# A 16-sequence attention and mixture-of-experts kernel on one core: three tiles combined to two turns of groups, the shared expert and the last routing steps placed elsewhere

## The reference

```python
x = x + attention(layernorm(x))        # 16 heads of 64, over 256 tokens, softmax, + bo
z = layernorm(x)
probs = sigmoid(z @ router_w.T + expert_bias)            # 160 experts
top_w, top_idx = top_k(probs, 8)
top_w = 2.5 * top_w / (sum(top_w) + 1e-09)
routed = sum over the 8 chosen e of  top_w[e] * (silu(z @ w_gate[e].T) @ w_down[e].T)   # inner size 64
shared = silu(z @ w_gate_shared.T) @ w_down_shared.T
out = x + routed + shared
```

## Time and profile before

| | us |
|---|---|
| median of 3 runs | 1121.14 |
| lowest and highest | 1119.48, 1123.74 |
| the profiled execution | 1122.37 |
| its span in the profile | 1120.5 |
| busy: PE, DVE, ACT, POOL | 868.7, 794.1, 703.0, 704.9 |
| granted PE clock, mean | 0.893 of full speed |

### The profile page before, as it was taken

One profiled execution on the slowest core, in us unless ns is written; L12 is line 12 of the kernel. 1 busy time (PEld: TensorE's weight loads), 2 busy tenths in 40 slices (PEclk: granted clock), 3 DMA queues, 4 the chain that ended last, 5 costly groups with the idle time before them and its releaser, 6 DMA issues.

```text
span 1120.5 us, 30801 instructions
## 1 busy us (share of the span) xinstructions
PE 868.7 (78%) x8800; PEld 673.4 (60%) x8800; DVE 794.1 (71%) x2741; ACT 703.0 (63%) x2069; POOL 704.9 (63%) x892
## 2 busy tenths in 40 slices
PE   5999999999999999999999977887775757700000
PEld 4777777777777778777777756665554535500000
DVE  4568888888888888888878888787775666743223
ACT  5888888888888888888888745764443434500000
POOL 2236676767767676776767755277555454577775
PEclk9999999999999999999999968998887887855555
DMA  8715644444443122312222446886665666522221
GB/s 266 313 59 225 261 164 162 176 183 183 173 184 109 63 94 68 104 60 103 70 75 84 143 155 214 261 284 218 213 202 166 189 197 190 177 61 54 61 56 49
DMA packets 75566, 170.00 MB, mean 152 GB/s; under 512 B 13809, under 2 KB 23985, under 8 KB 75505
## 3 DMA queue, kind: packets, MB, share of 16 engines
q1 hardware_dynamic: 56816, 133.63, 33.9%
q0 software_dynamic: 16384, 33.59, 10.4%
q10 hardware_dynamic: 2304, 2.10, 0.6%
HBM read 66.50 MB, written 102.76 MB: 151 GB/s over the span
## 4 chain that ended last, share of the span: by engine, by line
PE 61%; DVE 12%; POOL 10%; issue 10%; DVEq 5%; ACT 1%; DMA 0%; POOLq 0%; ACTq 0%
PE psS L419 12%; PE psO L494 11%; PE psT L444 9%; PE psY L410 9%; POOL yg L909 9%; DVE w_b L1253 6%; PE psVM L410 5%; PE psA L456 5%; DVEq L249 3%; PE psS L603 3%; PE psT L593 3%; PE psY L614 2%; DVE yg L1260 2%; DVEq L1253 1%; DVE yg L1262 1%
## 5 line engine op out<-in xcount | busy, mean ns | idle before, releaser
L909 POOL DMA_INDIRECT yg<-block_y,tok_idx x256 | 249.8, 976 | 167.2 <-issue 93.7
L883 POOL DMA_INDIRECT slot_x<-xn_src,slot_u x240 | 246.1, 1025 | 97.2 <-issue 54.8
L712 ACT ACTIVATE p_sb<-psS,negmax 128x256 f32<-128x256 f32 x512 | 236.0, 474 | 92.5 <-DVE negmax L1195 91.2
L1253 DVE COPY w_b<-w_all 128x192 f32 x832 | 171.0, 277 | 88.8 <-issue 49.4
L845 POOL TENSOR_SCALAR p_sb<-p_sb,rinv 128x256 f32<-128x256 f32 x256 | 137.3, 544 | 115.3 <-DVE rinv L1150 111.6
L1195 DVE TENSOR_REDUCE negmax<-psS 128x2 f32<-128x512 f32 x256 | 164.3, 683 | 28.6 <-PE psS L419 28.4
L419 PE MATMUL psS<-qk_sb 64*128 64x256 f32 x1024 | 145.2, 402 | 2.3 <-ACT p_sb L712 2.3
L494 PE MATMUL psO<-pT_sb,v_sb 128*64 128x256 f32 x1024 | 138.8, 390 | 4.1 <-issue 2.2
L287 ACT COPY pT_sb<-psT 128x512 f32<-128x512 f32 x256 | 140.9, 618 | 1.4 <-PE psT L444 1.4
L593 PE MATMUL psT<-ident,xb 128*128 128x128 f32 x416 | 80.2, 324 | 71.2 <-DVE x_res L1242 69.2
L444 PE MATMUL psT<-ident,p_sb 128*128 128x128 f32 x1024 | 132.7, 272 | 0.0
(11 more groups left out here) (164 smaller groups left out, 1796.5 us busy)
## 6 DMA issues: line engine op xcount, KB each, us to landing
block_y<-zero SPq DMA_DIRECT2D x26, 1024.0 KB
xb<-slot_x SPq DMA_DIRECT2D x104, 256.0 KB
block_y<-y_b SPq DMA_DIRECT2D x104, 256.0 KB
slot_x<-zero SPq DMA_DIRECT2D x15, 1024.0 KB, 4.0
w_all<-in_wgd_dram SPq DMA_DIRECT2D x16, 960.0 KB
slot_x<-zero SPq DMA_DIRECT2D x1, 11264.0 KB, 41.7
yg<-block_y,tok_idx POOLq DMA_INDIRECT x256
slot_x<-xn_src,slot_u POOLq DMA_INDIRECT x240
```

The source lines that it names most:

```text
L712: act.activation(p_sb[:, (g - 1) % 2, h, qt, :], psS[:, h, qt * SEQ:(qt + 1) * SEQ], ACT.Exp, bias=negmax[:, (g - 1) % 2, h, qt:qt + 1], s ...
L883: pool.indirect_dma_start(slot_x, bass.IndirectOffsetOnAxis(ap=slot_u[:, int(last), i, j:j + 1], axis=0), (xn2 if last else xn2_src)[:, i, ...
L909: pool.indirect_dma_start(yg[:, r, k, :], None, block_y, bass.IndirectOffsetOnAxis(ap=tok_idx[:, par, r, k:k + 1], axis=0)).then_inc(gat[r ...
L1253: m = dve.tensor_copy(w_b[:, RING - 1 - r, i, :], w_all[:, bass.ds(e, 1), :].rearrange("p o i -> p (o i)"))
```

## The change

`TILES_BY` says how many tiles are combined by the end of each turn from turn 10 on: 1, 3, 4, 6, ... 24. So turns have one and two `combine` in alternation, 24 are inside the turns and 8 behind them. All of DVE's turns from 7 on, and SP's from 8 on, are written out. The shared expert moves: `shared_hidden` to the turn's first group, `shared_out` to its second, DVE's `shared` behind the weights of the third group of the same turn, and PE's wait for it to the transposes of the third. SP's load of the shared expert's input comes a turn earlier. The last sequence's `chosen`, `best_places`, `blocks` and `weights` go from behind groups 7, 8 and 9 to behind groups 28 to 31; its table half from behind group 13 to behind group 33 (`LATE_TABLE`). `output_rows` now works on one sequence's 16 numbers per partition at a time, at step g = 6 of attention, with own small arrays; its last two calls come behind `ffn_norm(B)` and behind group 32. POOL's first gather waits only until 15 sequences have their row numbers; the third tile waits for the last sequence's row numbers and weights. In memory the tensors that the late steps still need lie where the third and fourth place of `yg` come.

```diff
+TILES_BY = [3 * j // 2 for j in range(TURNS - COMBINE_FROM + 1)]
-LEAD, LATE_RANKS, LATE_TABLE = 4, 5, 13
+LEAD, LATE_RANKS, LATE_TABLE = 4, 5, 33
...
-                    if r == 0 and chunk is not None:
-                        wait(pe, s["shared_ok"], chunk)
-                    if r == RING - 1 and chunk is not None:
+                    if r == 1 and chunk is not None:
                         pe.wait_ge(s["hs_ok"], chunk + 1)
+                    if r == 2 and chunk is not None:
+                        pe.wait_ge(s["shared_ok"], chunk + 1)
...
-                    if r == RING - 2 and chunk is not None:
+                    if r == 0 and chunk is not None:
                         shared_hidden(chunk)
-                    if r == RING - 1 and chunk is not None:
+                    if r == 1 and chunk is not None:
                         shared_out(chunk)
...
-            pool.wait_ge(s["wr_ok"], B)
-            pool.wait_ge(s["po_ok"], 3)
+            pool.wait_ge(s["po_ok"], SEALED + 1)
...
+                if isinstance(n, int) and n == 2:
+                    pool.wait_ge(s["wr_ok"], B)
+                    pool.wait_ge(s["po_ok"], B)
...
+            def output_rows(b):
+                n = b - 1
+                slot = slot_u[:, int(is_last(b, 2))]
                 wait(dve, s["su_ok"], n)
-                dve.tensor_copy(pos_u[:, bass.ds((b - 2) * TB, TB), :], slot_u[:, int(is_last(b, 2))]).then_inc(s["pu_ok"], 1)
+                dve.tensor_scalar(row_a[:], slot, 3, 6, ALU.bitwise_and, ALU.logical_shift_left).then_inc(s["pa_ok"], 1)
...
+                dve.tensor_tensor(pos_u[:, bass.ds((b - 2) * TB, TB), :], row_a[:], row_c[:], ALU.bitwise_or).then_inc(s["po_ok"], 1)
...
                         if g == 5:
                             weights(b)
+                        if g == 6:
+                            output_rows(b)
...
-                    if r == 0 and chunk is not None:
+                    if r == 2 and chunk is not None:
                         shared(chunk)
...
+            with dve.Fori(LEAD, COMBINE_FROM - 3) as it:
+                turn(it)
+            group(28)
             chosen(B + 1)
+            group(29)
             best_places(B + 1)
-            group(8)
+            group(30)
             blocks(B + 1)
-            group(9)
+            group(31)
             weights(B + 1)
-            group(10)
-            output_rows()
-            group(11)
-            group(12)
-            group(13)
+            group(32)
+            output_rows(B + 1)
+            group(33)
             dve.wait_ge(s["b_ps"], 2)
             table(psT[:, (LATE_TABLE - 1) % 2, :], TABLE_A, BC)
...
+            turn(COMBINE_FROM - 1, 0)
+            for j in range(TURNS - COMBINE_FROM):
+                turn(COMBINE_FROM + j, j + 1 if j + 1 < B else None)
+                for n in range(TILES_BY[j], TILES_BY[j + 1]):
+                    combine(n, n // YR, n % YR)
+            with dve.Fori(TILES_BY[-1] // YR, NT // YR) as q:
                 for k in range(YR):
                     combine(YR * q + k, q, k)
```

More of the change, by code:

```diff
@@ L135, in build @@
             newest = sa("newest", [P, E])
+            xn2T = sa("xn2T", [D, SEQ])
+            z_sb = sa("z_sb", [P, TB, E])
+            repl = sa("repl", [P, TB, E])
+            moved = repl
+            mask = sa("mask", [P, TB, E], BF16)
+            n_taken = sa("n_taken", [P, 1])
+            st2 = sa("st2", [P, TB, 6])
+            mv2 = sa("mv2", [P, TB, 2])
+            ve2 = sa("ve2", [P, TB])
+            rs2 = sa("rs2", [P, TB])
+            half = sa("half", [P, TB])
+            d = sa("d", [P, TB + 1, E])
+            le = d
+            taken = sa("taken", [P, E])
             placed = sa("placed", [P, TB, E])
+            score = sa("score", [P, TB, E])
             blk_num = sa("blk_num", [P, BC])
@@ L209, in build @@
         blk_i = sb("blk_i", [P, NBLK], I32)
+        tok_idx = sb("tok_idx", [P, 2, YR, TOPK], U32)
         w_all = sb("w_all", [P, E, INTER + D])
[L212 to L213 removed]
         xs = xn2_src[:].rearrange("p i d -> p (i d)")
@@ L357, in turn @@
                     store_y(RING * it + (r - STORE_LAG), (r - STORE_LAG) % 2)
-                    if r == 1 and chunk is not None:
-                        wait(sp, s["sh_ps"], chunk)
-                        sp.dma_start(xs, xT[bass.ds(chunk, 1)].rearrange("o p t -> (o p) t")).then_inc(s["xs_in"], 16)
+                if chunk is not None:
+                    wait(sp, s["sh_ps"], chunk)
+                    sp.dma_start(xs, xT[chunk]).then_inc(s["xs_in"], 16)
             xT = ffn_xT.rearrange("(b p) t -> b p t", p=D)
@@ L379, in _ @@
             sp.wait_ge(s["x2_st"], 16 * B)
[L380 to L392, removed]
+            for c in range(2):
+                turn(COMBINE_FROM - 2 + c, c)
+            for j in range(TURNS - COMBINE_FROM):
+                turn(COMBINE_FROM + j, j + 2 if j + 2 < B else None)
+                for n in range(TILES_BY[max(j - 1, 0)], TILES_BY[j]):
+                    store_out(n, n % YR)
             for n in range(NGRP - STORE_LAG, NGRP):
                 store_y(n, n % 2)
-            store_out(TURNS - COMBINE_FROM - 1, YR - 1)
-            with sp.Fori((TURNS - COMBINE_FROM) // YR, NT // YR) as q:
+            for n in range(TILES_BY[-2], TILES_BY[-1]):
+                store_out(n, n % YR)
+            with sp.Fori(TILES_BY[-1] // YR, NT // YR) as q:
                 for k in range(YR):
@@ L662, in _ @@
                 experts(it)
-            with pe.Fori(LEAD, COMBINE_FROM - 1) as it:
+            with pe.Fori(LEAD, COMBINE_FROM - 3) as it:
+                experts(it)
+            for it in range(COMBINE_FROM - 3, COMBINE_FROM - 1):
                 experts(it)
@@ L1284, in _ @@
             ffn_norm(B)
+            output_rows(B)
             dve.wait_ge(s["b_ps"], 1)
@@ L1318, in _ @@
             dve.wait_ge(s["tab_ok"], 2)
-            group(14)
-            group(15)
-            with dve.Fori(LEAD, COMBINE_FROM) as it:
-                turn(it)
-            for k in range(YR):
-                turn(COMBINE_FROM + k, k)
-                combine(k, 0, k)
-            with dve.Fori(1, (TURNS - COMBINE_FROM) // YR) as q:
-                for k in range(YR):
-                    turn(YR * q + (COMBINE_FROM + k), YR * q + k)
-                    combine(YR * q + k, q, k)
-            with dve.Fori((TURNS - COMBINE_FROM) // YR, NT // YR) as q:
+            group(34)
+            group(35)
+            turn(COMBINE_FROM - 1, 0)
+            for j in range(TURNS - COMBINE_FROM):
+                turn(COMBINE_FROM + j, j + 1 if j + 1 < B else None)
+                for n in range(TILES_BY[j], TILES_BY[j + 1]):
+                    combine(n, n // YR, n % YR)
+            with dve.Fori(TILES_BY[-1] // YR, NT // YR) as q:
                 for k in range(YR):
```

56 lines of the change are left out of this document (20 added, 36 removed).

## The result

The changed kernel takes 1074.76 us (median of 4 runs, 1074.22 to 1077.73), beside 1120.31 for the kernel before (4 runs): ratio 0.9597, 95% interval 0.9565 to 0.9629. The profiled execution has a span of 1072.4 us, where 1057 was forecast, and a mean granted clock of 0.912 (before 0.893). The time is inside the range of 1050 to 1076, by 1.2 us, and 17 us above the forecast of 1058.

The account below looks back on a forecast made before the run. POOL's gathers, waiting for DVE's sums, were taken as the bound. Tile 5 at 770.5, 275.4 for 27 tiles and 7.0 give 1052.9; 2 for attention and 2 for turns make 1057, median 1058 us, range 1050 to 1076.

Parts of the forecast that it names:

- rival (a): DVE's turns take above 15.1 us and set the end; about 1069 us at 16 a turn; chance 0.15.
- PE's waits for `x_res`: Sign: PE's waits for DVE's `shared` fall from 69.2 to under 30 us.
- A first gather near 714: Sign: POOL's gathers start near 714 us instead of 720.4.
- if a gather takes over 1.3 us: Sign that the prediction is wrong: a POOL gather over 1.3 us, where each took about 0.94.
- What bounds the kernel: POOL's gathers set the end, losing 67 us to waits for the sum of the tile four before.
- The first groups: Groups 7 to 13: moved steps save 6.2 us, table half 1.2, `output_rows(B)` costs 1.0; gathers start at 714.0.
- Attention: `output_rows` at g = 6 of 14 sequences: nothing or 0.6 us each, 8 us; 2 taken.
- The turns: DVE's turns: 12.1 us with one combine, 15.2 with two, mean 13.7, below POOL's 15.3.
- The sum: Tile 5 starts at 770.5; 27 tiles at 10.2 us are 275.4, plus 7.0 behind the last gather: 1052.9.
- (b): Groups 7 to 11 are bound elsewhere, gathers start at 719 to 720: 1061 to 1063 us; chance 0.07.
- (c): DVE's longer attention loop gets a gap at 11 jumps back, adding 44 us: 1100; chance 0.03.
- (d): POOL's gathers slow down beside DVE's copies, end near 1243 at the slowest gather seen; chance 0.02.

Follow-up runs that it names:

- g2_late_early: Changed kernel with the last sequence's steps and table half back behind groups 7 to 13; 1079.88 us, 0.9606 of the kernel before.
- g4_rows_only: Kernel before, with only `output_rows` on one sequence at a time at step 6 of attention; 1121.49 us, 0.9981 of the kernel before.
- f2_rows_behind_copy: Changed kernel with `output_rows` behind DVE's copy of psO at the end of step 5, second chip; 1072.25 us, 0.9527 of the kernel before.
- f3_no_multiply: Changed kernel without the multiplication by the routing weights in `combine`, second chip; 1064.02 us, 0.9465 of the kernel before.
- f4_all_three: Changed kernel with rows behind the copy, `combine` as eight multiply-adds, POOL written out without `tok_idx` copies; 1053.23 us, 0.9371 of the kernel before.
- e1_rows_behind_copy: Changed kernel with `output_rows` behind the copy of `oT_sb` in attention, on the slow first chip; 1269.99 us, 0.9901 of the kernel before.
- f1_after_again: Changed kernel as it is, run again on the second chip; 1073.79 us, 0.9546 of the kernel before.

## Why the prediction was right and where it was off

*The number.* That the time is in the range is in part luck. The forecast's own range was 1050 to 1064, and it was missed; 1064 to 1076 had been held open for the nearer half of rival (a), turns above 15.1 us, and they were 13.1. Of the signs that were named, PE's waits for `x_res` and the missing 5 us jumps of DVE came true. A first gather near 714, 10.2 us a tile and attention at most 3 us longer did not, and "if a gather takes over 1.3 us" was to show the prediction wrong: 18 of the 19 long ones do. That sign was badly chosen, as the 1989 ns of the earlier trace rows were there before.

*What bounds the kernel.* Right. POOL waited for the sum of the tile four before; with the sums early it runs almost without a wait for DVE from tile 6 to the end.

*The first groups.* Right: 7.9 us against 7.4; `g2_late_early` gives 6 for them at the first gather, and 5 to 6 at the end. `output_rows(B)` took 1.06 us (row 654.46 to 655.52 of DVE), 1.0 was taken. Not forecast were 1.7 us behind group 16, where loads for PE come late, and 2.0 more up to the first gather.

*Attention, the first step that failed.* "Bounds: nothing, or 0.6 each, 8 us. I take 2." The traces show 0.52 a sequence and 6.4 to 6.5 us from the first mask to the last, near the upper bound. PE full "means that it has work ahead" was the wrong reading, since a later maximum made every sequence longer. `g4_rows_only` gives 6.2 us for this step alone. Behind the copy 6.0 us are gone (`f2_rows_behind_copy`), of which 1.5 at most reach the end.

*The turns.* Right, and a little better than forecast: 12.1 and 15.2 us were given, mean 13.7; measured are 13.1 for the mean, and 11.2 with one combine. The third tile had its cover: `output_rows` ends at 737.2, its gather starts at 745.16. PE's waits for `x_res` fell to 18.2.

*The sum, the second step that failed.* "Tiles 5 to 31 are 27 x 10.2." The pace came from the earlier trace rows behind 991 us, where a multiplication starts only upon a landing and no copies run on DVE. Measured is 10.68 over the 27 tiles: 10.94 in the turns (tiles 5 to 23), 10.07 behind them. The 27 tiles hold 10.6 us of long gathers, where the 12 tiles of the earlier trace rows held 1.6, or 3.5 in 27: 7.1 of the 13.1 us are theirs. The gaps at the `tok_idx` copy hold 7.5, the 12 tiles 1.1, or 2.5 in 27: 5.0 more. The last 1.0 is spread over all gathers. `f3_no_multiply` takes a part of the first out, and `f4_all_three` both: a tile is then 10.06. The signs were in the trace of before, the 1989 ns of the earlier trace rows and nine gathers over 1.1 us. Three of these (in tiles 3, 4 and 14) lay ahead of a wait of POOL for DVE, which hid them; three lay in the very stretch that gave the 10.2.

*The rivals.* (a) did not happen on the chips of the main runs, with turns of 13; on the first chip of the experiments it did, with 23.4 in `e1_rows_behind_copy`, and all of the gain but 1% was gone. What (b) feared, a start that doesn't come earlier, happened, though for another reason and further than it gave: 724.04 and not 719 to 720, because attention was later and more was lost behind group 16, not because groups 7 to 11 were bound elsewhere. (c) did not happen. (d) was named for the copies and priced for all gathers; what happened is its small form, by an instruction with two inputs in SBUF, for 17 gathers.

The Trainium skill's page "SBUF — State Buffer", section "Who interferes with whom", states that a DVE instruction with two SBUF inputs contends with a GpSimd instruction that reads SBUF. The traces agree: a gather, which reads its indices there, starting beside such an instruction ends 0.82 us after it. Copies, which by the same section of the Trainium skill can contend with GpSimd too, do not show it here: 92 gathers of the changed kernel start while one runs, with a mean of 955 ns, beside 948 for those behind 1000 us, where no copies run, and only one of the 92 is long.

## What to carry to other kernels

When a wait goes away, read the pace of the next bound engine in the stretch where the others will be busy beside it, and count its longest instructions there too: what was hidden behind the wait is now paid. Here 1.3 us of small operations put ahead of the maximum in a softmax cost 0.5 us in each round although PE was full, and next to nothing behind a copy; ask what stands behind the place, not only which engine is full. Try the parts of a change by themselves: two that cure the same wait don't add up, and the second is spare until the pace is raised.

## What the runs showed of the hardware

- A gather of POOL that starts while a DVE instruction with two SBUF inputs runs ends 0.82 to 0.83 us after that instruction, so up to 1.9 us instead of 0.94. With none but short ones in `combine` (at most 0.39 us) no gather was above 1.1.
- An earlier start can be lost again on PE: with attention 4.5 us earlier (`f2_rows_behind_copy`), the granted clock from 726 to 756 us was between 0.62 and 0.81 in four of five windows of 6 us, where `f1_after_again` had 1.00, and the lead was gone at the first combine. PE had waited 2 to 3 us ahead of each fall. That the waits or the early start caused the falls was not tried, and two kernels with the late start fell too.
- The 5.3 us at a loop's jump back are not a property of the loop's length: with other code ahead of the same loop they were gone, and with them the packets of the instruction queue in that stretch. Which placement makes them was not tried.
- One chip needs 1283 us for the kernel that takes 1120 to 1124 in all other runs, with PE's instructions arriving in pieces; versions of the change are between 1% faster and 0.6% slower than before there.
